# Feed-forward's first weights, their parts and two turned batches moved into the attention's last group

## The reference: what is computed

```python
x = x + batch_product_fp8(layernorm(x), ctx, mask)
x = x + experts(layernorm(x), shared 2, routed 16, top 2)
x = x + attention(layernorm(x), ctx, Wq, Wk, Wv, Wo)       # 16 heads of 128
x = x + W2 . fwht(silu(W1 . h) * (W3 . h)),  h = layernorm(x)   # 2048 hidden
```

## Time and profile before

| | us |
|---|---|
| median of 3 runs | 2170.0 (2169.38 to 2171.07) |
| profiled execution, its own time | 2165.98 |
| its span (first to last instruction) | 2164.4 |
| attention's last group and the tail | about 1530 to 1602 of the span |
| feed-forward | 1602.75 to the end |

### The profile page before, as it was taken

How to read it: one execution, slowest core, us unless ns; L and a number is a source line. 1 busy time by engine, 2 the same in 40 slices (tenths; PEclk the granted TensorE clock), 3 DMA queues, 4 the chain that set the end, 5 groups by cost and what they waited for, 6 DMA issues and landing times. The chain is left out here.

```text
span 2164.4 us, 29041 instructions
## 1 busy us (share of the span) xinstructions
PE 2011.6 (93%) x9849; PEld 1667.8 (77%) x9849; DVE 1320.8 (61%) x2071; ACT 841.6 (39%) x1638; POOL 866.3 (40%) x741
## 2 busy tenths in 40 slices
PE   4989599994899999999999999999968999999998
PEld 4777477773778888888888888888856888888887
DVE  7975258887777766668676666666556333333333
ACT  4532148883444444444544444444422111111111
POOL 1103200003577766667766566666551222202200
PEclk9978799997999999999999999999999999999999
DMA  7365249994566666566555555555531111001002
GB/s 284 122 239 214 106 145 393 390 376 156 175 185 183 182 170 187 163 191 178 164 163 161 153 152 167 168 148 148 144 114 34 30 29 30 20 10 29 0 1 78
DMA packets 170271, 323.70 MB, mean 150 GB/s; under 512 B 16064, under 2 KB 41536, under 8 KB 170176
## 3 DMA queue, kind: packets, MB, share of 16 engines
q1 hardware_dynamic: 155072, 272.12, 40.4%
q0 software_dynamic: 15104, 50.34, 7.3%
HBM read 210.73 MB, written 111.67 MB: 149 GB/s over the span
## 5 line engine op out<-in xcount | busy, mean ns | idle before, releaser
L1360 POOL TENSOR_TENSOR t_pT_lo<-t_pT_raw,t_pT_hi 128x512 fp32r<-128x512 f32 x256 | 327.5, 1299 | 221.0 <-ACT t_pT_hi L1456 219.4
L1555 DVE TENSOR_REDUCE t_sums<-t_score 128x1 f32<-128x512 f32 x256 | 169.8, 688 | 130.9 <-PE t_score L52 129.4
L1918 DVE TENSOR_TENSOR f_lin<-f_lin,f_silu 128x512 f32<-128x512 f32 x64 | 44.7, 700 | 289.7 <-PE f_lin L52 289.7
L1471 ACT ACTIVATE t_probs<-t_score,t_sums 128x512 f32<-128x512 f32 x256 | 174.8, 683 | 82.8 <-DVE t_sums L1555 64.7
L1545 DVE STREAM_TRANSPOSE t_blocks<-t_probs 128x512 f32<-128x512 f32 x256 | 172.7, 693 | 22.5 <-ACT t_probs L1471 22.2
L1537 DVE SCALAR_TENSOR_TENSOR x_res<-t_out,t_sums,x_res 128x512 f32<-128x512 f32 x256 | 179.1, 741 | 4.0 <-PE t_out L52 4.0
L1456 ACT ACTIVATE t_pT_hi<-t_pT_raw 128x512 fp32r<-128x512 f32 x256 | 160.2, 626 | 3.8 <-DMA t_pT_raw<-turned_blocks 3.5
L1843 POOL TENSOR_TENSOR f_w_hi<-w_raw,f_zeros 128x1024 fp32r<-128x1024 f32 x16 | 30.5, 1904 | 319.5 <-PE f_gate L52 314.8
L1876 ACT ACTIVATE f_silu<-f_gate 128x512 f32<-128x512 f32 x64 | 38.3, 598 | 303.3 <-PE f_gate L52 303.3
L1450 ACT ACTIVATE t_o_hi<-t_o 128x512 fp32r<-128x512 f32 x64 | 38.3, 598 | 226.9 <-PE t_o L52 226.9
L52 PE MATMUL t_score<-t_wv_hi,t_cT_hi 128*128 128x256 f32 x416 | 117.6, 283 | 0.7 <-ACT t_probs L1471 0.7
(11 more groups left out here) (287 smaller groups left out, 6090.2 us busy)
## 6 DMA issues: line engine op xcount, KB each, us to landing
turned_blocks<-t_blocks SPq DMA_DIRECT2D x256, 256.0 KB
t_pT_raw<-turned_blocks SPq DMA_DIRECT2D x256, 256.0 KB, 4.0
e_up_raw<-in_L_ffn_Wrt_up_dram SPq DMA_DIRECT2D x47, 512.0 KB, 6.5
e_down_raw<-in_L_ffn_Wrt_down_dram SPq DMA_DIRECT2D x47, 512.0 KB, 6.0
tokens_by_expert<-e_xg SPq DMA_DIRECT2D x1, 12032.0 KB, 41.0
e_xg<-tokens_by_expert SPq DMA_DIRECT2D x47, 256.0 KB, 6.2
outputs_by_expert<-e_y_out SPq DMA_DIRECT2D x47, 256.0 KB, 6.3
wq_raw<-in_L_xattn_Wq_dram POOLq DMA_DIRECT2D x32, 256.0 KB, 4.6
```

The lines of the kernel that those rows point to most:

```text
L1360: pool.tensor_tensor(pT_lo[:, q], pT_raw[:, q], f32(pT_hi[:, q]), ALU.subtract).then_inc(p_ready, 1)
L1471: act.activation(probs[:, t % 2, :], score_bank[t][:, :], ACT.Exp, bias=neg_max[:, t:t + 1], accum_out=inv[:, p, t:t + 1]).then_inc(exp_re ...
L1555: dve.tensor_reduce(neg_max[:, t:t + 1], score_bank[t][:, :], AX.X, ALU.max, negate=True).then_inc(max_ready, 1)
L1918: dve.tensor_tensor(lin_bank[k][:, :], lin_bank[k][:, :], silu[:, k, :], ALU.mult).then_inc(mid_done, 1)
```

## The change

Five things move from the feed-forward's start into the attention's last group. **Loads:** SyncE issues the first W1, W3 and W2 loads (512 KB each) and the Hadamard matrix (64 KB) behind the move of unit 60, into buffers that are dead by then (W1 and W3 into the context's raw tiles, W2 into the raw tile of Wv, the Hadamard matrix into that of Wq). **Splits:** GpSimd splits W1 and W2 between low(61) and low(62), behind a wait for the last q product; ScalarE and VectorE split W3, and ScalarE copies the Hadamard matrix, behind unit 63. **Batch 0** (nth 4): VectorE normalises it at the end of unit 62, TensorE turns it in unit 63 ahead of weigh(62), ScalarE and VectorE split it ahead of the head output of unit 62. **Batch 1** (nth 5): VectorE normalises it ahead of that same head output; TensorE turns it between output(62) and weigh(63); VectorE splits it, behind the row statistics of batch 2, ahead of the head output of unit 63. **Stores:** the last batch goes out in four stores of 256 KB, each behind its own addition, instead of one of 1 MB. The split results lie where the attention's x and context parts were, in the places where the feed-forward expects them.

```diff
+class FfnEntry:
+    def __init__(self, nc, ctx):
+        self.size = 6 * KD * GH + P + 4 * KD * S
+        places = ExitStack()
+        al = Alloc(nc, places, "entry")
+        self.up_hi = [al.sb(f"w{n}_hi", [KD, GH], F32R) for n in (1, 3)]
...
+        self.xT_lo = [al.sb(f"xT_lo{b}", [KD, S], F32R) for b in range(2)]
+        places.close()
...
 # attention, SyncE, group
                     move(4 * g + p, p)
+                    if known(g) and g == PAIRS * GROUPS - 1 and p == 0:
+                        group_weights.load(sp, "1", 0)
+                        group_weights.load(sp, "3", 0)
+                        sp.wait_ge(w_ready["v"], PAIRS * GROUPS)
+                        group_weights.load(sp, "2", 0)
+                        sp.wait_ge(w_ready["q"], PAIRS * H)
+                        sp.dma_start(w_raw["q"][:, 0, :], had_in).then_inc(entry.had_loaded, 16)
...
 # attention, GpSimd, group
                 low(r, n + 1, after=("o", h1 - 1))
-                if not final:
+                if final:
+                    pool.wait_ge(q_done, LAST + 1)
+                    ffn_up()
+                    ffn_w2()
+                else:
...
 # attention, ScalarE
             run_groups(act, group)
+            act.wait_ge(group_weights.loaded["3"], 16)
+            act.wait_ge(entry.up_hi_ready, 1)
+            act.activation(entry.up_hi[1][:], group_weights.raw["3"][:, :, :], ACT.Copy).then_inc(entry.up_hi_ready, 1)
+            act.wait_ge(entry.had_loaded, 16)
+            act.activation(entry.had[:, :], w_raw["q"][:, 0, :], ACT.Copy).then_inc(entry.had_ready, 1)
+            act.wait_ge(k_done, LAST + 1)
+            act.wait_ge(v_done, values_made(PAIRS - 1, PAIRS * GROUPS - 1, 3))
+            ln.scalar_hi(act, 4, entry.xT_hi[0], 0)
             head_output(LAST - 1)
             for q in range(Q4):
                 turned(LAST, q)
+            ln.scalar_hi(act, 5, entry.xT_hi[1], 0)
             head_output(LAST)
...
 # attention, VectorE, unit and tail
+                if known(n) and n == LAST - 1:
+                    ln.vector_norm(dve, 0, 4)
...
-            for n, p in ((LAST - 1, 2), (LAST, 3)):
-                head_output(n)
-                for t in range(TB):
-                    add(PAIRS - 1, n, p, t)
+            dve.wait_ge(entry.up_hi_ready, 2)
+            dve.wait_ge(entry.up_ready, 1)
+            dve.tensor_tensor(entry.up_lo[1][:], group_weights.raw["3"][:, :, :], f32(entry.up_hi[1][:]),
+                              ALU.subtract).then_inc(entry.up_ready, 1)
+            ln.vector_lo(dve, 4, entry.xT_hi[0], entry.xT_lo[0], 0)
+            ln.vector_norm(dve, 1, 5)
+            head_output(LAST - 1)
+            for t in range(TB):
+                add(PAIRS - 1, LAST - 1, 2, t)
+            dve.wait_ge(added, LAST * TB)
+            stats.read(dve, 2)
+            ln.vector_lo(dve, 5, entry.xT_hi[1], entry.xT_lo[1], 0)
+            head_output(LAST)
+            for t in range(TB):
+                add(PAIRS - 1, LAST, 3, t)
...
 # attention, TensorE, unit and tail
+                if last:
+                    ln.tensor_turn(pe, 4, bank_free=lambda t: pe.wait_ge(exp_ready, n * TB + t + 1))
                 if not first:
                     weigh(n - 1, 1 - b, (1, 0, 0, 1)[p], 4 * g + (0, 2, 4, 4)[p])
...
             output(LAST - 1, 0, PAIRS * H, range(TB))
+            ln.tensor_turn(pe, 5, bank_free=lambda t: pe.wait_ge(ln.lo_ready, 4 * TB + t + 1))
             weigh(LAST, 1, 1, 2 * PAIRS * H)
...
 # feed-forward, SyncE
-            for name in "132":
-                group_weights.load(sp, name, 0)
-            sp.dma_start(had_raw[:, :], had_in).then_inc(had_loaded, 16)
...
-            for b in range(B):
+            for b in range(B - 1):
...
+            for t in range(TB):
+                sp.wait_ge(added, (NG * B - 1) * TB + t + 1)
+                sp.dma_start(out[B - 1, t * P:(t + 1) * P, :], x_res[:, TB * (B - 1) + t, :]).then_inc(stored, 16)
...
 # feed-forward, GpSimd, ScalarE, VectorE, TensorE
-            split(0, 0, True)
             split(1, 1, True)
...
-            ln.scalar_hi(act, 0, xT_hi, 0)
-            act.wait_ge(had_loaded, 16)
-            act.activation(had[:, :], had_raw[:, :], ACT.Copy).then_inc(had_ready, 1)
-            unit(0, 0, lambda: ln.scalar_hi(act, 1, xT_hi, 1))
+            unit(0, 0)
...
-                        stats.compute(dve, 2, 2)
+                        stats.read(dve, 3)
+                        stats.finish(dve, 2, 2)
...
-            ln.vector_norm(dve, 0, 0)
-            ln.vector_lo(dve, 0, xT_hi, xT_lo, 0)
-            ln.vector_norm(dve, 1, 1)
-            unit(0, 0, lambda: ln.vector_lo(dve, 1, xT_hi, xT_lo, 1))
+            unit(0, 0)
...
-            ln.tensor_turn(pe, 0)
-            pe.wait_ge(ln.lo_ready, TB)
             up(0, 0, 0, 0)
-            ln.tensor_turn(pe, 1)
-            pe.wait_ge(had_ready, 1)
+            pe.wait_ge(entry.had_ready, 1)
```

More of the change, by code:

```diff
@@ L134, with __init__ @@
 class RawWeights:
-    def __init__(self, nc, ctx, shapes, slices):
+    def __init__(self, nc, ctx, shapes, slices, places=None):
         self.slices = slices
-        self.raw = {n: ctx.enter_context(nc.sbuf_tensor(f"w{n}_raw", [P] + shape, F32)) for n, shape in shapes.items()}
+        self.raw = places or {n: ctx.enter_context(nc.sbuf_tensor(f"w{n}_raw", [P] + shape, F32))
+                              for n, shape in shapes.items()}
         self.loaded = {n: ctx.enter_context(nc.semaphore(f"w{n}_in")) for n in shapes}
@@ L144, in load @@
         src = self.slices[n]
-        sp.dma_start(self.raw[n][:], src[index] if isinstance(index, int) else src[bass.ds(index, 1)]
+        sp.dma_start(self.raw[n][:, :, :], src[index] if isinstance(index, int) else src[bass.ds(index, 1)]
                      ).then_inc(self.loaded[n], 16)
+class FfnEntry:
[4 more added lines that the diff above has]
+        self.up_hi = [al.sb(f"w{n}_hi", [KD, GH], F32R) for n in (1, 3)]
+        self.up_lo = [al.sb(f"w{n}_lo", [KD, GH], F32R) for n in (1, 3)]
+        self.w2T_hi, self.w2T_lo = al.sb("w2T_hi", [KG, D], F32R), al.sb("w2T_lo", [KG, D], F32R)
+        self.had = al.sb("had", [P], F32R)
+        self.xT_hi = [al.sb(f"xT_hi{b}", [KD, S], F32R) for b in range(2)]
+        self.xT_lo = [al.sb(f"xT_lo{b}", [KD, S], F32R) for b in range(2)]
+        places.close()
+        sem = lambda name: nc.alloc_semaphore(f"entry_{name}")
+        self.up_hi_ready, self.up_ready = sem("up_hi_ready"), sem("up_ready")
+        self.w2_hi_ready, self.w2_ready = sem("w2_hi_ready"), sem("w2_ready")
+        self.had_loaded, self.had_ready = sem("had_in"), sem("had_ready")
 class LayerNorm:
@@ L1792, in hadamard_ffn_phase @@
         zeros = al.sb("zeros", [KD])
-        had_raw, had = al.sb("had_raw", [P]), al.sb("had", [P], F32R)
         gate_bank = [al.ps(f"gate{k}", [S]) for k in range(KG)]
@@ L1976, in up @@
                         three_pass(pe, bank[:, :], lambda c: up_hi[i][kind][:, c, ks],
-                                   lambda c: up_lo[i][kind][:, c, ks], lambda c: xT_hi[:, c, cols],
-                                   lambda c: xT_lo[:, c, cols], KD).then_inc(done, 1)
+                                   lambda c: up_lo[i][kind][:, c, ks], lambda c: xT_hi[b][:, c, :],
+                                   lambda c: xT_lo[b][:, c, :], KD).then_inc(done, 1)
             def group(g, i, start, last):
@@ L1982, in group @@
                     u = g * B + b
-                    if start and b + 1 < B:
-                        pe.wait_ge(ln.lo_ready, TB * (b + 2))
+                    if start and 0 < b < B - 1:
+                        pe.wait_ge(ln.lo_ready, TB * b)
                     if b + 1 < B:
```

71 lines of the change are left out of this document (45 added, 26 removed).

## The result

| | before | after |
|---|---|---|
| median, us | 2169.53 (10 runs) | 2153.89 (10 runs) |
| range, us | 2163.69 to 2171.07, and one of 5161.22 | 2147.63 to 2160.17 |
| profiled execution, us | 2165.98 | 2148.4 |
| its span, us | 2164.4 | 2146.8 |

The ratio is 0.994, with a 95% interval from 0.9923 to 0.9956; it leaves out the slow execution of 5161.22 us. That is some 13 us won (9.5 to 16.7; the two medians stand 15.6 apart), where the prediction had 7.6. The direction and the mechanism were the forecast's; the size was not.

A forecast was written before the change was run, and what follows sets the result against it. TensorE, busy 93%, was taken as the bound, with winnable waits at the attention/feed-forward seam. 5.6 us at up(1) plus 2.0 from stores gave 7.6 off 2170.0, so 2162.4 us; range 2155 to 2166.5.

The forecast's parts named there:

- Loads, cost nothing: SyncE's queue between the moves of units 60 and 61: the loads fit in 10 us, cost 0 (bounds 0 and +1).
- rival D: SyncE's queue: loads and waits delay the move of unit 61; slower, 2176 us at 24 us between moves; chance 0.04.
- GpSimd's splits, no delay to low(62): GpSimd between low(61) and low(62): W1 and W2 splits take 8.6 us and fit by 2.2 us.
- Batch 0 held up by them, 1.5 us: VectorE at unit 62's end: normalising waits on GpSimd's splits, making unit 63 1.5 us late (bounds 0 and 2.5).
- Turning, W3's low part and the subtractions: Attention's tail: 16 transposes on TensorE 2.1 us; on VectorE, W3's low part 1.8 (1.2 to 2.5), four subtractions 2.8.
- The normalising of batch 1: VectorE ahead of unit 62's head output: one slips in, others wait beside low(63); 1589.9 to 1595.0 (bounds 1591.8 and 1596).
- output(62) and output(63) late by 8.6 and 9.7: TensorE in the attention's tail: output(62) starts at 1595.8 instead of 1587.17, output(63) at 1607.4 instead of 1597.68.
- Rival C: Start of up(0): first matmuls again at 1.2 GHz, 2.25 us less won, 2164.6 us; chance 0.20.
- up(1) directly behind up(0), gap 1.5: Feed-forward's start: up(1) follows up(0)'s end after 1.5 us, at 1624.9 instead of 1630.53, 5.6 us won.
- The stores, 2.0: End of the kernel: 256 KB last stores land sooner than one of 1 MB, 2.0 us won (bounds 1 and 2.5).
- Rival B: Attention's tail: normalising not held up, output(63) 2.9 late, up(1) 12.4 us earlier, 2155.6 us; chance 0.16.
- A: The forecast itself: the seam's 17 us of waiting go, some 10 return as a longer tail; chance 0.49.

The follow-up runs named there:

- repeats: The kernel after, unaltered, measured twice more: medians 2150.46 and 2154.86 us, ratios to the kernel before 0.9916 and 0.9953.
- run 5: Against the kernel after: VectorE normalises batch 0 one unit earlier, in unit 61; 2124.51 us, ratio to before 0.9928.
- run 10: Against the kernel after: GpSimd's split of W2 behind low(62) instead of ahead of it; 2156.41 us, ratio to before 0.9961.
- 3: Against the kernel after: batch 1 normalised behind the head output of unit 62 instead of ahead; 2152.64 us, ratio to before 0.9936.
- 8: Against the kernel after: batch 0 normalised in unit 61 and turned before output(61), batch 1's normalising and batch 2's statistics behind head outputs; ratio to before 0.994.
- Run 6: Against the kernel after: batch 0 turned ahead of output(61) instead of behind it; 2129.41 us, ratio to before 0.9938.
- run 9: Against the kernel after: both batches back in the feed-forward, only weight loads, splits and stores stay moved; 2157.24 us, ratio to before 0.9958.
- run 1: Against the kernel before: only the last batch's four stores of 256 KB; 2164.75 us, ratio to before 0.9991.
- run 4: The kernel after once more, nothing changed; 2150.46 us, ratio to before 0.9916.
- run 12: The kernel after a third time, nothing changed; 2154.86 us, ratio to before 0.9953.
- run 11: Against the kernel after: both batches normalised early, W2 split and batch 2's statistics later, batch 1 turned before output(62); 2149.44 us; M (unit 60's last additions to up(1)) 45.9.

## Why the prediction was right and where it was wrong

Starts in us behind the last additions of unit 60 (the forecast's own times less 1569.94):

| | before | forecast | after | repeats |
|---|---|---|---|---|
| output(61) | 8.1 | 9.6 | 9.4 | 9.4, 9.4 |
| low part of head output 62 | | 25.1 | 21.5 | 22.1, 22.1 |
| output(62) | 17.2 | 25.9 | 22.2 | 22.9, 22.9 |
| output(63) | 27.7 | 37.5 | 33.3 | 34.8, 34.8 |
| up(0) | 42.2 | 42.6 | 37.9 | 40.5, 40.5 |
| up(1) | 60.6 | 55.0 | 50.5 | 53.1, 53.2 |

**Loads, cost nothing: right.** The queue row shows it, and with it rival D falls.

**GpSimd's splits, no delay to low(62): right**, from 1560.14 to 1568.84. **Batch 0 held up by them, 1.5 us: right.** Its four took 3.81, output(61) came 1.3 later, and run 5, which takes the meeting away, gives just these 1.3 back.

**Turning, W3's low part and the subtractions: near.** Forecast 2.1, 1.8 and 2.8; measured 1.91, 1.56 and 2.47. For W3 I had weighed the Trainium skill (SBUF — State Buffer, section SBUF: two separate sides). Its rule is an exclusive lock: whichever of the two operations starts first keeps the shared ports for its whole length. The traces agree, with one turn that I had missed: in the kernel after VectorE had only the rest of GpSimd's copy to wait for (1.56 in all) and was then ahead of GpSimd's subtraction, so GpSimd paid (2.16 for 1.29). In run 10 a longer subtraction of GpSimd's, W2's, was under way, and VectorE's took 2.79, which is above my upper bound of 2.5.

**The normalising of batch 1: this is the step that failed, in its size.** The prediction had one normalisation slip in ahead and the others wait a piece each, "done at 1595.0", 5.1 us from 1589.9. It took 2.85: three slipped in ahead, and one waited. VectorE was 1.16 us ahead of low(63), where I had 0.6. Of the 3.6 us by which the head output of unit 62 came sooner than forecast (21.5 to 25.1), 2.3 are this term; the rest are 0.3 for W3, 0.4 for the subtractions and 0.6 for the additions ahead of them. The mechanism itself is shown by four kernels in which VectorE came after low(63) had started:

| kernel | normalising starts behind low(63) by, us | it takes, us | its end behind low(63)'s start, us |
|---|---|---|---|
| after (and the repeats) | -1.16 (-1.15, -1.13) | 2.85 (2.86, 2.86) | 1.7 |
| 3 | 0.05 | 5.75 | 5.8 |
| 10 | 0.08 | 5.68 | 5.8 |
| 8 | 0.28 | 5.52 | 5.8 |
| 6 | 0.64 | 5.12 | 5.8 |

In the four lower rows the end does not depend on when VectorE came: its four operations take turns with the four of low(63), most of them 1.48 us each instead of 0.53. It hangs on who is first, by a margin of a us; my sum for VectorE up to there was 1.3 us too long and the one for low(63) 0.7. The price of 5.1 did not follow from my own margin either: normalisations start some 0.5 us apart, so in 0.6 us two slip in ahead and two wait. By the table that is some 3.7 us (an estimate: one wait ends at 1.7, four at 5.8, so two at 3.1, and 0.6 ahead of it). Run 6 came to 5.12 with VectorE late, which is another case; that the figures agree is chance.

**output(62) and output(63) late by 8.6 and 9.7: right in kind, 5.0 and 5.5 in the kernel after and 5.7 and 7.1 in the repeats.** In the repeats VectorE was 3.0 us ahead of the forecast at the head output of unit 62, and 1.1 of these were gone at up(1), 0.6 of it where output(63) ran at half clock (5.7 us from there to up(0), 5.1 in the forecast); the kernel after kept its 3.6 and had 0.9 more (4.6 us there). So two of the signs that the prediction had named did not come: the second four over 4 us, and output(62) some 8 late.

**Half clock in output(62), full clock in up(0): right.** Rival C had up(0) start at 1.2 GHz. Its first twelve took 3.00. In run 9 most of C came true (1.7 us of its 2.25), with the transposes of batch 0 right ahead of up(0) and idle time on both sides of them. The rule of the Trainium skill by which I had weighed C (TensorE: Matmul & The Clock Gate, Part 4: PE-mode transpose) fits that run, but so does the idle time alone; no run here tells the two apart.

**up(1) directly behind up(0), gap 1.5: right, 1.44** (1615.84 - 1614.40). **The stores, 2.0: 2.3**, shown alone by run 1.

**Rival B** (normalising not held up, 12.4 us at the seam) was half true: batch 1 was mostly free, batch 0 was not. The seam gave 10.1 in the profiled execution and 7.5 in the two repeats, which lie between A's 5.6 and B's 12.4.

**The sum.** By parts the change is worth 7.5 + 0.6 + 2.3 = 10.4 us in the repeats and 13.0 in the kernel after's own trace. The ratios say 13 (9.5 to 16.7), 18 (11 to 25) for run 4 and 10 (6.3 to 14.3) for run 12. Of the kernel after's 13.0 the forecast of 7.6 lacks 5.4: 2.3 for the normalising, 1.3 for the other work of VectorE up to the head output, 0.9 behind it, 0.6 in the feed-forward and 0.3 in the stores. Of the repeats' 10.4 it lacks 2.8, as the two terms of VectorE's gave 3.0 there and 1.1 of it was lost again. The range held the ratio because it reached down to rival B's time, not because the sum was close. The rest of the raw 17.6 between the two profiled executions is not the change.

## What to carry to other kernels

Work moved into idle time is free only where its operations don't meet those of the other engine of the pair VectorE and GpSimd: here four normalisations cost 1.9 alone and 2.9 or 5.8 us by a margin of one us, so lay the two timelines side by side, ask which comes first, and where that hangs on one us price both cases and let the range hold them. An edit that takes one such wait away moves the next meeting too (runs 3, 8 and 10), and the kernel that put both batches' normalising where GpSimd is idle, at the price of a buffer, had a shorter M than any order beside it (run 11, which moved other things as well). Where only the landing of the last store is left, splitting it by tiles gives 2.3 us for nothing.
